# Attention and mixture of experts on one core: seven of eight blocks of the middle stage moved into the attention's steps

## What is computed

```python
def xattn(query, key, values, mask, W_out):        # 16 heads of 32, 128 keys
    energy = einsum('nqhd,nkhd->nhqk', q, k)
    energy = where(mask == 0, -1e20, energy)
    attn = softmax(energy / sqrt(512), axis=-1)
    return einsum('nhqk,nkhd->nqhd', attn, v).reshape(N, Q, 512) @ W_out.T

def ffn(x, proj_w, anchors, routing_temp, w1, w2):  # 6 experts of width 256, top 2
    z = einsum('btd,ed->bte', x, proj_w)
    q = tanh(z / 0.3)
    logits = -((6.0 - einsum('btd,ed->bte', q, anchors)) * 0.5) / clip(routing_temp, 0.1)
    topk_logits, topk_idx = top_k(logits, 2)
    expert_weights = scatter of softmax(topk_logits) to topk_idx
    h = gelu(einsum('btd,edh->bteh', x, w1))
    return einsum('bteh,ehd,bte->btd', h, w2, expert_weights)

x = x + xattn(layernorm(x), ctx, ctx, mask, W_out)   # x: 2 x 2048 x 512, float32
x = x + ffn(layernorm(x), proj_w, anchors, routing_temp, w1, w2)
```

## Time and profile before

| | |
|---|---|
| three runs | 753.84 us median, 751.01 to 757.17 |
| profiled execution | 750.03 us, span 748.3 us |
| mean granted TensorE clock | 0.909 of 2.4 GHz |
| busy: PE, DVE, ACT, POOL | 618.3, 454.8, 323.4, 283.7 us |
| moved by DMA | 142.93 MB |

### The profile page before, as it was taken

The page is one execution under the profiler, slowest core; times in us unless marked ns, Lnnn a source line. Parts: engine busy times, 40 slices in busy tenths (PEclk is TensorE's granted clock), DMA queues, the critical chain, the costliest instruction groups (busy, mean ns, idle before and its releaser), DMA issues.

```text
span 748.3 us, 15304 instructions
## 1 busy us (share of the span) xinstructions
PE 618.3 (83%) x4628; PEld 471.2 (63%) x4629; DVE 454.8 (61%) x972; ACT 323.4 (43%) x616; POOL 283.7 (38%) x414
## 2 busy tenths in 40 slices
PE   5989999999986988999853779999999999998000
PEld 3765555555523766776643768999999888887000
DVE  4857777776644648778762445555555667766465
ACT  4547767777674355545331223333333333332000
POOL 5425545554353247776674200000001222322674
PEclk9779999999998999999955798999999999999555
DMA  5311222212313686999737435665565888887686
GB/s 172 98 33 67 87 94 93 89 68 69 131 72 140 220 289 236 307 337 349 287 151 263 164 133 191 196 194 181 190 195 180 275 291 281 272 277 252 211 277 230
DMA packets 71529, 142.93 MB, mean 191 GB/s; under 512 B 8742, under 2 KB 11814, under 8 KB 71468
## 3 DMA queue, kind: packets, MB, share of 16 engines
q1 hardware_dynamic: 61228, 108.58, 43.1%
q0 software_dynamic: 10240, 33.56, 13.7%
HBM read 77.63 MB, written 64.49 MB: 190 GB/s over the span
## 4 chain that ended last, share of the span: by engine, by line
PE 46%; issue 16%; DMA 9%; DVE 9%; POOL 8%; SPq 4%; ACT 4%; another core or an unknown queue 2%; DVEq 1%; POOLq 0%; ACTq 0%
PE ps L1359 6%; DMA y_d<-ysb 6%; PE ps L1372 4%; PE ps L1421 3%; PE ps L1522 3%; PE ps L1523 3%; PE ps L1524 3%; PE ps L1543 3%; PE ps L1544 3%; PE ps L1545 3%; PE ps L1511 2%; PE ps L1392 2%; POOL yg L730 2%; PE ps L1438 2%
## 5 line engine op out<-in xcount | busy, mean ns | idle before, releaser
L730 POOL DMA_INDIRECT yg<-y_d,sidx x64 | 64.5, 1008 | 256.7 <-DVE wst L1211 222.8
L975 DVE TENSOR_REDUCE nmax<-ps 128x4 f32<-128x512 f32 x128 | 82.3, 687 | 54.0 <-PE ps L1359 54.0
L1522 PE MATMUL ps<-w1H,xgH 128*128 x296 | 91.4, 309 | 3.0 <-DVE xgL L1232 2.9
L893 ACT ACTIVATE xgH<-ps 128x512 fp32r<-128x512 f32 x74 | 44.3, 599 | 110.2 <-PE ps L1511 97.6
L791 ACT ACTIVATE prob<-ps 128x512 f32<-128x512 f32 x128 | 66.1, 602 | 48.6 <-PE ps L1375 48.6
L1524 PE MATMUL ps<-w1L,xgH 128*128 x296 | 85.0, 287 | 0.0
L1523 PE MATMUL ps<-w1H,xgL 128*128 x296 | 84.9, 287 | 0.0
L1359 PEld LDWEIGHTS ps<-kfT,qT 32*128 32x128 f32 x1024 | 68.2, 198 | 18.6 <-issue 9.5
L1359 PE MATMUL ps<-kfT,qT 32*128 32x128 f32 x1024 | 75.3, 290 | 2.8 <-DVE nmax L975 2.3
L1245 DVE COPY ysb<-ps 128x512 f32<-128x512 f32 x74 | 51.1, 690 | 43.3 <-PE ps L1545 23.4
L710 POOL DMA_INDIRECT xs_d<-x,place_now x64 | 63.7, 996 | 29.7 <-issue 20.5
(11 more groups left out here) (193 smaller groups left out, 1297.3 us busy)
## 6 DMA issues: line engine op xcount, KB each, us to landing
xg<-xs_d SPq DMA_DIRECT2D x74, 256.0 KB, 3.1
y_d<-ysb SPq DMA_DIRECT2D x74, 256.0 KB
xin<-in_x SPq DMA_DIRECT2D x32, 256.0 KB, 2.7
att_d<-atT SPq DMA_DIRECT2D x32, 256.0 KB, 2.0
atL<-att_d SPq DMA_DIRECT2D x16, 512.0 KB
x<-in_x SPq DMA_DIRECT2D x32, 256.0 KB
x_d<-x SPq DMA_DIRECT2D x32, 256.0 KB
x2t<-x_d SPq DMA_DIRECT2D x16, 256.0 KB, 2.7
```

Of the source, the lines that this page charges most:

```text
L730: nc.gpsimd.indirect_dma_start(yg[:, k, z, :], None, y_d[b], bass.IndirectOffsetOnAxis(ap=sidx[:, k, z:z + 1], axis=0))\
L975: nc.vector.tensor_reduce(nmax[:, n % 2, :, g * hpg + h], ps[:, token_bank(v, h), :].rearrange("p (t k) -> p t k", t=4), axis=AX.X, op=ALU ...
L1522: mm(o, xgH[:, p, c, :], w1h[:, cols], start=(c == 0), stop=False)
```

## The change

The loop `attention_loop` now goes to S_LAST = L_MID + 4 * INSIDE - 1 = 44, with L_MID = 17 and INSIDE = 7: a step s from 17 on is quarter q of iteration i = (s - 17) // 4 and carries the work of row tile q of it. `middle_loop` keeps i from 7 to 10. Inside, one PSUM bank each is used for the projection (3), the transposed rows (2) and the router (1), which are banks of the key scores; so the projection waits for the step's exponentials, and the next key scores wait for the reads of those banks. att_d is gone: ScalarE makes atH straight from atT and VectorE makes atL from atT and atH, a group of heads at a time, a step after atT. The weights, whose memory the attention uses to its end, all move behind it.

```diff
+        INSIDE, I_OUT, I_T2, I_Z = nblk - 1, 3, 2, 1
...
+        L_SPLIT, L_MID = L_DIV + 1, L_DIV + 5
+        L_ROWS, L_T2 = L_MID - 2, 1
+        S_LAST = L_MID + 4 * INSIDE - 1
...
-            for s in range(L_LOAD, ntile + L_DIV):
+            for s in range(L_LOAD, S_LAST + 1):
                 body(s)
...
-        W_AT = (0, 1, 1, 1, 2, 2, 2, 3, 4, 5, 6, 7)
+        W_AT = (7, 7, 7, 7, 8, 8, 8, 8, 9, 9, 10, 10)
...
-            for i in range(nblk + 3):
+            for i in range(INSIDE, nblk + 3):
                 body(i)
```

```diff
-                    sp.dma_start(att_d[n, g, :, :], atT[:, v % 2, :]).then_inc(at_out[g], 16)
...
+                w = s - L_ROWS
+                if live(w, ntile):
+                    load_row(w // 4, w % 4)
+                w = s - L_MID
+                if live(w, ntile):
+                    store_rows(w // 4, w % 4)
...
+            sp.wait_ge(atL_done, ntile)
             middle_loop(sp, middle)
```

GpSimd, VectorE and ScalarE in a step:

```diff
+                i, q = quarter(s)
+                if q == 0:
+                    row_factors(i - 1)
...
+                i, q = quarter(s)
+                scatter(i - 3, q)
...
+                if q == 0 and live(i - 3, nblk):
+                    shares(i - 3)
+                if q == 3 and live(i - 2, nblk):
+                    router_logits(i - 2)
+                if i >= 0:
+                    residual(i, q)
+                if q == 3:
+                    moments(i)
+                    if live(i - 2, nblk):
+                        places(i - 2)
                 if live(v, ntile):
                     maxima(v, 1)
+                u = s - L_SPLIT
+                if live(u, ntile):
...
+                    nc.vector.tensor_tensor(atL[:, n % 2, g, :], atT[:, u % 2, :], atH[:, n % 2, g, :], ALU.subtract)\
+                      .then_inc(atL_done, 1)
...
+                w = s - L_MID - 4
+                if live(w, ntile):
+                    normalise(w // 4, w % 4)
...
+                    nc.scalar.activation(atH[:, n % 2, g, :], atT[:, u % 2, :], ACT.Copy).then_inc(atH_done, 1)
+                w, count = rows_turned(s)
+                for z in range(count):
+                    if live(w + z, ntile):
+                        rows_out((w + z) // 4, (w + z) % 4)
+                if q == 1:
+                    logits_part(i - 2)
+                if q == 2:
+                    squash(i - 2)
+                if q == 3:
+                    exponentials(i - 2)
```

```diff
+                if q == 1 and live(i - 2, nblk):
+                    pe.wait_ge(zp_done, i - 1)
+                if q == 2 and live(i - 2, nblk):
+                    pe.wait_ge(q_done, i - 1)
+                if q == 3 and live(i - 2, nblk):
+                    pe.wait_ge(used_done, i - 1)
+                after(pe, t2_done, rows_turned(v + L_KEY)[0])
+                after(pe, add_done, v + L_KEY - L_MID)
...
+                i, q = quarter(s)
+                if i >= 0:
+                    if live(k, ntile):
+                        pe.wait_ge(exp_done, hpg * (k + 1))
+                    project(i, q)
+                w, count = rows_turned(s)
+                for z in range(count):
+                    if live(w + z, ntile):
+                        rows_transposed((w + z) // 4, (w + z) % 4)
+                if q == 1:
+                    logits_part(i - 2)
+                if q == 2:
+                    logits(i - 2)
+                if q == 3:
+                    prefix(i - 2)
```

More of the change, by code:

```diff
@@ L688, in middle @@
             def middle(i):
[L689 to L711, removed]
-                                x2[:, n % 4, t, :], None).then_inc(scattered[n % 2][t], 16)
+                row_factors(i - 1)
+                for t in range(4):
+                    scatter(i - 3, t)
                 for e, z, j in weights_at(i):
@@ L877, in middle @@
+                for t in range(4):
+                    rows_out(i - 1, t)
                 for e, z, j in weights_at(i):
@@ new lines, in _, with middle @@
+            attention_loop(attention)
+            def middle(i):
+                residual(i, 0)
+                n = i - 2
+                if live(n, nblk):
+                    router_logits(n)
+                for t in range(1, 4):
+                    residual(i, t)
+                moments(i)
+                if live(n, nblk):
+                    places(n)
+                    shares(n)
+                if i == blk_per_batch + 3:
+                    rows_of_tiles(0)
+                    table(0)
+                if i == blk_per_batch + 4:
+                    rows_of_tokens(0)
@@ L1376, in scores_by_key, with project @@
                         .then_inc(sc_ready, 1)
+            def project(n, t):
+                if live(n, nblk):
+                    if t == 0:
+                        pe.wait_ge(atH_done, 4 * n + 4)
+                        pe.wait_ge(atL_done, 4 * n + 4)
+                    if n < INSIDE:
+                        after(pe, add_done, 4 * n + t)
+                    elif n == INSIDE and t == 0:
+                        pe.wait_ge(exp_done, hpg * ntile)
+                        pe.wait_ge(qT_done, ntile)
+                        pe.wait_ge(add_done, 4 * n)
+                        pe.wait_ge(t2_done, 4 * (n - 1))
+                        pe.wait_ge(used_done, n - 2)
+                    o = ps[:, out_bank(n, t), :]
+                    h, l = atH[:, n % 2, :, t * P:(t + 1) * P], atL[:, n % 2, :, t * P:(t + 1) * P]
+                    for g in range(kchunks):
+                        mm(o, h[:, g, :], woH[:, g, :], start=(g == 0), stop=False)
+                        mm(o, h[:, g, :], woL[:, g, :], start=False, stop=False)
+                        last = mm(o, l[:, g, :], woH[:, g, :], start=False, stop=(g == kchunks - 1))
+                    last.then_inc(out_ready, 1)
@@ new lines, in logits_part @@
+            def logits_part(n):
+                if live(n, nblk):
+                    pe.wait_ge(t2_done, 4 * n + 4)
+                    after(pe, zp_done, n)
+                    if n + 2 == INSIDE:
+                        pe.wait_ge(newton_done, ntile)
+                        pe.wait_ge(raw_done, ntile)
+                    for c in range(kchunks):
+                        last = mm(ps[c * HD:(c + 1) * HD, zp_bank(n), :], projT[:, c, :], x2T[:, :, c, :], start=True, stop=True)
+                    last.then_inc(zp_ready, 1)
```

375 lines of the change are left out of this document (178 added, 197 removed).

## The result

The changed kernel takes 776.72 us (median; 774.78 to 779.85, four runs) against 752.42 us for the kernel before (749.11 to 757.17). The ratio is 1.0322, with a 95% interval of 1.0253 to 1.039: slower by 24 us. The profiled execution has a span of 778.1 us, against 748.3. Ratios here compare only runs in the faster of two states that a kernel's executions show, while medians are over all runs.

The account below looks back on a forecast made before the run. The prediction took TensorE, with its loop through VectorE and ScalarE about level, to bound the attention, and GpSimd's queue the tail. -4 + 26.4 - 5 = +17.4 gave 767.5 or 771 by base; it said 769, range 747 to 797.

Parts of the forecast that it names:

- the likeliest case: The whole kernel: the forecast of 769 us itself, with its own range 758 to 783; chance 0.55.
- The loop of TensorE and VectorE: Attention steps from 17: denominators, transposes, projection, a drain, seven VectorE operations and semaphores make one turn 9.7 us.
- Step 41 at 328: End of the attention: from 86.66 us, blocks 0 to 5 sum to 241 us, so step 41 starts at 328.
- Block 4's 38.7: Attention steps of block 4: 38.7 us, with no new rows to normalise or transpose, 2.4 us less.
- Another 24 from step 41 to the last block: After step 41: exponentials and newton 8, denominators 1, three groups of projection, transposes and routing at about 5 each.
- gain: 4: Attention and middle stage: the last block's projection starts at 352 instead of 355.88, 4 us gained.
- Table loads, 1 us a block: ScalarE in the attention: 30 more table loads over 15 steps, 1.31 us a switch, charged at 1 us a block.
- The tail, 77: Last block's projection to experts: GpSimd's scatters, subtractions, norm factors and a wait take 77 us, 26.4 more than before.
- 5 us back at the experts' start: First experts: scatters are out before they start, so 5 us of earlier waiting come back, bounds 0 and 11.
- Rival 2: Attention: ScalarE becomes the bound, table loads costing twice 1.31 us, +26 to +36, 795 to 805 us; chance 0.13.
- Rival 1: Attention: TensorE stays packed, last projection starts at 330 to 340, total 744 to 759 us; chance 0.2.
- Rival 3: Attention: in-order queues lock, a microsecond in each of 28 steps, +28, 797 us; chance 0.12.

Follow-up runs that it names:

- kernel 5: The changed kernel with the subtraction that makes atL back on GpSimd from VectorE: 772.1 us, ratio 1.0485 to the kernel before.
- the second trace: Profile of the changed kernel run again, unedited, on another chip: 776.64 us, ratio 1.0304 to the kernel before.
- kernel 2: The changed kernel with one table set for logarithm and exponential loaded behind each Tanh inside the attention: 765.3 us.
- kernel 1: The kernel before with the expert weights in the tail as in the changed kernel, no middle stage moved: 757.15 us, ratio 1.0264.
- 8: The kernel before with the weights in the tail and their subtractions on VectorE, no middle stage moved: 733.62 us, ratio 0.9965.
- 9: The kernel before with the weights' subtractions on VectorE, at their old places: 741.32 us, ratio 0.9865.
- kernel 3: The changed kernel with the weights' subtractions on VectorE instead of GpSimd: 753.1 us, ratio 1.0235 to the kernel before.
- kernel 7: The changed kernel with three edits: weights' subtractions on VectorE, one logarithm and exponential table set, atL's split on GpSimd for the first three blocks: 741.39 us, again 739.55.

## Why the prediction was right, and where its sizes were off

**The sum.** Forecast 769, measured 776.7, inside the likeliest case's own range of 758 to 783. The mechanism was right as well: the tail's queue, with little won ahead of it. In the profile: +17.4 forecast, +29.8 found (778.1 against 748.3); against medians +24.3.

**The loop of TensorE and VectorE, 9.7 us: right in kind, 0.6 too long.** Steps 18 to 20 take 9.08, and kernel 5 shows that the split stands in the loop. VectorE's seven operations were counted at 0.69 each; in the trace they start 0.6 to 0.7 apart (two maxima take 1.27 together), and denominators with transposes take 1.41 (110.25 to 111.66) instead of 1.6.

**Step 41 at 328: found at 332.1 and 329.2.** Some of this is luck, since errors cancel: blocks 0 and 1 took 76.1 us in the second trace instead of 78.8, and blocks 3 and 4 took 85.5 instead of 82.2. Block 4's 38.7 can't be had from the forecast's own terms either (43.5 less 2.4 is 41.1, and 41.2 was found). In the first trace step 17 starts 1.6 later than before, at 88.3, and one step takes 14.1 us, from 206.7 on (11.8 in the second). There the windows have the granted clock at 0.50 to 0.53, about the lower level, 1.2 GHz:

```profile
206.00:210.00 4.00, 4.00 (x30) 2.21 (x24) 2.78 (x6) 0.77 (x2) 2.29 (x6) 0.53 0.08 31
210.00:214.00 4.00, 4.00 (x24) 2.11 (x21) 3.06 (x6) 2.83 (x6) 2.63 (x6) 0.50 0.02 4
```

**Another 24 from step 41 to the last block: 30.4 and 28.8.** This is the step that failed by size. "About 8 for Exp and newton" was 10.0 (332.06 to 342.08), of which TensorE's timeline has 2.09 as a wait of the denominators for newton, below. The rest was 16 by the forecast and is 20.4 and 18.8, since the last of the "three groups at about 5" is 8.4 in both traces (349.6 to 358.0 in the second trace): the prefix count, the router's logits and the last atL stand there ahead of the last block.

```profile
342.08 1.29 PE L1513 MATMUL ps<-prob,ones 128*32 128x512 f32 x8 [2.09 <-DVE newton L1143]
```

So the last block was due at 352 and came at 362.5 and 358.0; "gain: 4" was a loss of 2 to 7 against 355.9.

**Table loads, 1 us a block: 5.1 us in 13 steps for those that kernel 2 takes away.** 13 steps were charged with 3.3. The price of one, 1.31, was right, and their count, 33. Rival 2 is out: without 20 of the loads the steps fall by 0.4.

**The tail, 77: 78.6 and 79.5, and 76.4 in kernel 1, where it stands alone.** The parts: 10.0 us for eight scatters (forecast 10.15), subtractions at 2.33 to 2.37 (forecast 2.39 and 2.64, 28 instead of 30), and 3.88 instead of 2 for ScalarE's first cast. "Loss in the tail 26.4" is 28 to 29.

**5 us back at the experts' start: 4.8** (778.1 - 441.1 = 337.0, against 748.3 - 406.5 = 341.8).

**What the forecast didn't price.** It compared the moved stage with the stage of the kernel before, 121 us long, and took its waits as its own. Kernels 1, 8 and 9 show that 12 to 17 us of them came from the weights' work among the iterations, which the change takes out as well. Against the same weights in the tail, moving the stage loses 10.1 us on one chip (346.8 in kernel 1, 356.9 in kernel 3, whose edit stands behind), and 3.7 with all edits, also on one. So the change loses twice: the tail, and steps that cost more inside than the stage did behind them.

**Rival 1** (packed, 330 to 340) did not come; the nearest, kernel 7, has its last block at 345.5 to 347.4. **Rival 3** (a microsecond in each of 28 steps) neither.

## What to carry to other kernels

When work is moved under a busy engine, price two kernels beside the changed one: the old order with everything that the move displaces already displaced, and the new one without it. Here the displaced weights alone gave a ratio of 1.026, and the stage itself ran better left alone. In a tail, add up the queue of the engine that releases the next stage, and then name what comes next behind it: taking 28 us of subtractions out gave 22 and brought a wait for DMAs to light, and turning two pieces of the queue round gave almost nothing, since one had been covering another engine's lateness. And compare with a kernel run on the same chip.

## What the hardware showed that was not expected

A small VectorE operation took as long as four of GpSimd's. In the tail of the changed kernel the 48 elements of pick took 9.82 us, where they take 0.20 elsewhere, and ended when GpSimd's four subtractions, 400.25 to 409.49, were over:

```profile
399.74 9.82 DVE L1057 TENSOR_TENSOR pick<-rank,rank 128x48 f32<-128x48 f32 x1 [0.23 <-issue]
409.49 0.17 DVE L1061 SCALAR_TENSOR_TENSOR wsel<-rank,lexp 128x24 f32<-128x24 f32 x1
```

The scatter that waits for it (410.53) lost 1.04 us; the second trace has 9.81 us for the same operation. With the subtractions on VectorE it takes 0.20 us. The Trainium skill (SBUF — State Buffer, SBUF: two separate sides) says that the two engines share a port pair that one holds for a whole instruction while the other is blocked; the rows agree. They add that VectorE may not get in between subtractions in a row. It does at other times: beside the four subtractions before these, from 378.25 to 387.51, one VectorE operation ended with each, as in these rows of VectorE's timeline.

```profile
380.61 2.35 DVE L1061 SCALAR_TENSOR_TENSOR wsel<-rank,lexp 128x24 f32<-128x24 f32 x1
382.88 2.40 DVE L1063 TENSOR_TENSOR pslot<-pick,slot 128x48 f32<-128x48 f32 x1
```

Why one operation had to wait for four isn't shown by these runs.

The same subtraction of 128x1024 elements takes 2.35 us on GpSimd and 1.23 on VectorE:

```profile
375.94 1.23 DVE L1121 TENSOR_TENSOR w1L<-w1L,w1H 128x1024 fp32r<-128x1024 f32 x1
```

The granted clock fell to half in the middle of the attention, at 206 us, after a stretch at 1.00 in which TensorE was busy for 35.3 of 36 us (170 to 206); in the second trace it was 0.85 from 202 to 206 and 0.73 from 206 to 210. What started it isn't shown by these runs. And the kernel before itself ran at 736 us on two chips and at 753 on three, a difference two thirds as large as the one studied; the cause of its part behind the experts' start, 9 us, stays open.
